# A GNN kernel's far tiles: one fused add and maximum per shared slot, and finer counts for GpSimd's lists

## The reference

```
h = relu(layernorm(x));  x = x + L0(h, adj)        # weighted mean of neighbours, times W
h = relu(layernorm(x));  x = x + L1(h, adj)        # hyperbolic mean
h = relu(layernorm(x));  x = x + L2(h, adj)        # maximum over 32 neighbours (below)
h = relu(layernorm(x));  x = x + L3(h, adj)        # hyperbolic mean with inverse roots of row sums

# L2
h = einsum('ni,oi->no', x, W) + b
_, topk_idx = top_k(adj, 32)          # the 32 largest entries of each row of adj
h_agg = max(h[topk_idx], axis=1)      # 8192 x 128
```

## Time and profile before

| | us |
|---|---|
| median of 3 runs | 3620.86 (3619.2 to 3623.95) |
| the profiled execution's own time | 3622.68 |
| its span, first to last instruction | 3620.9 |
| PE busy | 3338.5 (92%) |
| DVE busy | 2551.1 (70%) |
| POOL busy | 2505.2 (69%) |
| ACT busy | 1607.9 (44%) |
| gathers L508, own lists, whole program | 630.5, 624 instructions, 1010 ns each |
| rests L519 | 211.2, 485 instructions |

### The profile page before, as it was taken

How to read it: one execution, slowest core, us unless ns; L and a number is a source line. 1 busy time by engine, 2 the same in 40 slices (tenths; PEclk the granted TensorE clock), 3 DMA queues, 4 the chain that set the end, 5 groups by cost and what they waited for, 6 DMA issues and landing times.

```text
span 3620.9 us, 77053 instructions
## 1 busy us (share of the span) xinstructions
PE 3338.5 (92%) x29444; PEld 3316.9 (92%) x29444; DVE 2551.1 (70%) x5491; ACT 1607.9 (44%) x3554; POOL 2505.2 (69%) x2509
## 2 busy tenths in 40 slices
PE   6999999999999999999999999960899998999894
PEld 6999999999999999999999999960899998999894
DVE  6688888888888888530147656557787877878767
ACT  5777887887887887331222212222111111212124
POOL 3999998998998998200087666755787778778400
PEclk9999999999999999999999999985999999999997
DMA  6999999999999999888899999961788998889781
GB/s 211 393 397 389 387 379 367 385 382 361 390 382 367 388 386 365 312 292 293 289 342 331 327 329 333 329 233 39 268 306 303 321 323 305 296 310 337 269 291 57
DMA packets 401362, 1155.53 MB, mean 319 GB/s; under 512 B 36717, under 2 KB 56110, under 8 KB 401006
## 3 DMA queue, kind: packets, MB, share of 16 engines
q1 hardware_dynamic: 360096, 1082.21, 82.2%
q0 software_dynamic: 31360, 64.29, 5.8%
q10 hardware_dynamic: 9550, 4.69, 0.4%
HBM read 874.19 MB, written 276.86 MB: 318 GB/s over the span
## 4 chain that ended last, share of the span: by engine, by line
PE 65%; DVE 13%; POOL 12%; issue 5%; DMA 2%; ACT 2%; POOLq 0%; DVEq 0%; ACTq 0%; SPq 0%
PE psU L668 21%; PE psT L752 19%; PE psT L656 10%; POOL D L508 7%; PE psU L752 6%; PE psT L784 6%; POOL idle_end L519 2%; PE psU L784 2%; DVE agg L1695 2%; POOL ATS L508 2%; DMA adj_turned<-ATS 2%; DVE D L1482 1%; DVE HT L1691 1%; DVE W L1695 1%; DVE GR L1854 1%
## 5 line engine op out<-in xcount | busy, mean ns | idle before, releaser
L500 POOL TENSOR_TENSOR D<-D,iota 128x512 f32<-128x512 f32 x1024 | 1311.3, 1313 | 105.1 <-ACT D L911 83.9
L668 PE MATMUL psU<-HB,ATS 128*128 128x129 f32 x8192 | 1005.9, 276 | 18.7 <-ACT ATS L904 15.8
L668 PEld LDWEIGHTS psU<-HB,ATS 128*128 128x128 f32 x8192 | 957.0, 192 | 27.8 <-ACT ATS L904 19.9
L784 PE MATMUL psT<-ATS,PIECES 128*128 128x129 f32 x6144 | 787.3, 279 | 140.1 <-ACT ATS L1070 74.0
L784 PEld LDWEIGHTS psT<-ATS,PIECES 128*128 128x128 f32 x6144 | 741.4, 195 | 145.5 <-issue 113.4
L1482 DVE MAX8 D<-D 128x8 f32<-128x512 f32 x1024 | 643.0, 683 | 238.8 <-POOL D L500 231.0
L752 PE MATMUL psT<-GR,PIECES 128*128 128x129 f32 x6144 | 769.9, 275 | 1.1 <-issue 1.1
L508 POOL DMA_INDIRECT D<-h_table,idx_own x624 | 630.5, 1010 | 149.1 <-issue 101.4
L752 PEld LDWEIGHTS psT<-GR,PIECES 128*128 128x128 f32 x6144 | 727.2, 192 | 1.3 <-issue 1.3
L904 ACT ACTIVATE ATS<-psT 128x512 f32<-128x512 f32 x1024 | 555.7, 596 | 255.9 <-PE psT L656 208.5
L911 ACT ACTIVATE D<-PIECES 128x1024 f32<-128x1024 f32 x512 | 543.8, 1062 | 31.7 <-DVE D L1482 31.7
(11 more groups left out here) (411 smaller groups left out, 2739.1 us busy)
## 6 DMA issues: line engine op xcount, KB each, us to landing
PIECES<-adj_turned SPq DMA_DIRECT2D x512, 1024.0 KB
PIECES<-in_adj SPq DMA_DIRECT2D x256, 1024.0 KB
adj_turned<-ATS SPq DMA_DIRECT2D x512, 512.0 KB, 7.7
D<-h_table,idx_own POOLq DMA_INDIRECT x624
h_table<-HB ACTq DMA_DIRECT2D x8, 512.0 KB, 6.6
D<-h_table,idx_pool POOLq DMA_INDIRECT x215, 2.5
out_x<-X SPq DMA_DIRECT2D x3, 1024.0 KB, 5.1
ATS<-h_table,idx_pool POOLq DMA_INDIRECT x117
```

The costliest lines, as they stand in the source:

```text
L500: pool.tensor_tensor(key, key, iota[:, :], ALU.mult).then_inc(keyed, 1)
L668: last = nc.tensor.matmul(sum4(r), AT[K % NAT][:, b * GROUP + r * P:b * GROUP + (r + 1) * P], HB[:, j, :], start=(j == 0 and r % 2 == 0), ...
L784: last = nc.tensor.matmul(acc(h, r), block_of(slot, b, r), Hc[par][:, jj, :], start=(jj == 0 and opens(r)), stop=(jj == CT - 1 and closes(r)))
```

## The change

1. `far_tile` no longer reads n or branches. For each of the 22 slots, used or not, one SCALAR_TENSOR_TENSOR adds the mask's column to the slot and takes the maximum with an accumulator, alternately `gmax` and `pmax`; each waits for the one before last (`settle`). One maximum joins the two. Unused slots hold an earlier group's rows and are masked.
2. `pool_gathers` chooses its leaf by a binary tree of branches instead of a cascade; the far lists of groups 1 to 15 have twelve counts, `FAR_COUNTS`, instead of four. The near lists and the early group's keep their counts.

```
+FAR_COUNTS = [9, 10, 11, 12, 13, 14, 15, 16, 17, 18, 20, FAR_POOL]
...
-                if len(cuts) == 1:
-                    leaf(cuts[0])
-                    return
-                with pool.If(n < cuts[0] + 1):
-                    leaf(cuts[0])
-                with pool.Else():
-                    pool_gathers(ring, rows, index, n, cuts[1:], done, so_far, held)
+                def branch(counts):
+                    half = len(counts) // 2
+                    if not half:
+                        leaf(counts[0])
+                        return
+                    with pool.If(n < counts[half - 1] + 1):
+                        branch(counts[:half])
+                    with pool.Else():
+                        branch(counts[half:])
+
+                branch(cuts)
...
-                pool_gathers(far_pools[par], table, idx_pool[par], n, FAR_CUTS, far_pool_gathered[par],
+                pool_gathers(far_pools[par], table, idx_pool[par], n, FAR_COUNTS, far_pool_gathered[par],
...
-                n = dve.value_load(CTL[0:1, 1, g:g + 1], min_val=1, max_val=FAR_POOL)
+                ring, mask, best = far_pools[par], keep[par][:, r, :], (gmax, pmax)
                 dve.wait_ge(x_ready, t)
                 if r == 0:
                     dve.wait_ge(far_pool_gathered[par], 16 * FAR_POOL * ((g + 1) // 2))
                 dve.sem_inc(carrier["dve"], 1)
-                parts_max(t, n, FAR_CUTS, far_pools[par], far_kept, keep[par][:, r, :], gmax,
-                          NT + t * (TURNS // 2), NT + t * TURNS)
-                dve.wait_ge(pool_reduced, NT + (t + 1) * TURNS)
-                dve.sem_inc(carrier["dve"], 1)
+                for k in range(FAR_POOL):
+                    if k >= 2:
+                        settle(st.k - 1)
+                    mark(v.scalar_tensor_tensor(best[k % 2], ring[:, k, :], mask[:, k:k + 1],
+                                                best[k % 2] if k >= 2 else AGG[:, t, :], ALU.add, ALU.max))
+                settle()
+                link(v.tensor_tensor(gmax, gmax, pmax, ALU.max))
                 v.tensor_tensor(X[:, t, :], X[:, t, :], gmax, ALU.add).then_inc(x_ready, 1)
```

More of the change, by code:

```diff
@@ L225, in build @@
         KEPT = 2 * GROUP // P
-        far_kept = HT[:, :, :].rearrange("p b x -> p (b x)").rearrange("p (k f) -> p k f", f=P)
         gmax, pmax = agg4[:, 0, :], agg4[:, 1, :]
```

## The result

The changed kernel takes **3723.98 us** (median of 4 runs, 3718.65 to 3732.67) against 3620.43: ratio 1.0288, 95% interval 1.0269 to 1.0307. It is 103 us slower where 21 us faster were forecast. The profiled executions of the two kernels, from which their rows come, took 3719.05 and 3622.68, 96 us apart.

The account below looks back on a forecast made before the run. VectorE was taken to bind at long lists, with GpSimd a near second bound. GpSimd's last gather: 3402 - 16.8 - 20 + 48 = 3413, or 3409 chunk by chunk; so -21 us, 3600 us, range 3550 to 3642.

Parts of the forecast that it names:

- The bounds: Last stage: VectorE binds at long lists; GpSimd, 60.1 us a group against PE's 57.2, is only just ahead.
- the 79.2 us: Last stage: TensorE's time waiting, 32 times, for VectorE to free a PSUM buffer.
- Part 1, the merge: VectorE's far tiles: chain pitch 0.262 us, 7.8 us a tile for every list length, against 7.35 to 11.6.
- Rival C: VectorE's chain runs one after another, tile 10.5 us, VectorE binds in every chunk: +51, 3673 us; chance 0.05.
- Part 2, the lists: GpSimd's shared far lists: 218 gathers instead of 230, 1.40 us each, -16.8 us.
- Part 3, port contention: GpSimd's own gathers beside VectorE: fewer held as the long adds go, -20 us (between 0 and -33).
- Rival D: Port pair held through each VectorE chain: a gather waits some 4 us, 60 tiles, +240, about 3850 us; chance 0.02.
- Part 4, the jumps: GpSimd's list exits and entries: longer jumps over unused leaves miss instruction fetch, +48 us (bounds 0 and 103).
- The sum's method: Last stage: books of three engines kept chunk by chunk put GpSimd's last gather at 3409, the end at 3473 us.
- own gathers' mean under 1.0: Sign of being right: GpSimd's own gathers in the last stage average under 1.0 us, from 1.033.
- the wait on L784's buffers: Sign of being right: last-stage wait for PSUM buffers falls from 79 to under 20 us.
- gathers of 3 us or more (D): Sign of being wrong: GpSimd gathers taking 3 us or more, pointing to the port held through each chain.

Follow-up runs that it names:

- breaks6: Changed kernel with every sixth instruction of a tile's merge chain waiting for the one directly before it; 3612.87 us, ratio 0.9981.
- lists_only: Kernel before the change with only the finer list counts and the branch tree added, VectorE merging as before; 3640.23 us, ratio 1.0068.
- tails_psum: Changed kernel with merge accumulators in PSUM and the first 9 shared gathers placed ahead of the branch tree; 3541.82 us, ratio 0.9787.
- psum_acc: Changed kernel with the merge's two accumulators moved from SBUF to PSUM, tree and lists kept; 3602.87 us, ratio 0.9954.
- cuts_psum: Changed kernel with accumulators in PSUM and the old far lists (four counts, cascade of branches); 3564.88 us, ratio 0.9850.

## Why the prediction was wrong, point by point

- **The bounds** were read rightly, but for the 79.2 us, which count some waits twice: GpSimd just ahead of PE, VectorE binding at long lists. "The gain of a faster merge is soon capped by it" is what happened.
- **Part 1, the merge**: right. Pitch 0.262 forecast, 0.263 measured; tile 7.8 forecast, 7.71 measured, for every list. The 0.19 us an instruction estimated from the Trainium skill (page "VectorE: DVE Perf Modes", section on the TRN2 errata) is not what this chain shows. Rival C, a serial chain, is out. One reading was wrong without harm here: twelve instructions in 3.50 us are (3.50 - 0.345)/11 = 0.287 apart, not "the same" as 0.262. It does harm in part 3. (0.345 and 0.262 were each worked out from the other; the sixteen of the other chain last 0.346 us each and begin 0.262 apart.)
- **Part 2, the lists**: right. -16.8 us forecast; 218 shared gathers as counted from the inputs, and 15 us less of plain gather time.
- **Part 3, port contention: the step that failed.** Forecast -20 us, between 0 and -33; measured +94. GpSimd's last gather was put at 3413 and began at 3527, 114 us later, and this term alone was 114 us off. I rested it on one gather of 0.99 us beside a chain at 1950. That chain is not one row. The 0.287 above are pauses: the twelve stand in three rows of four, each 1.14 to 1.15 us long (two of them here), with a break before the next like those of breaks6.

```profile
1950.26 1.14 DVE L1647 SCALAR_TENSOR_TENSOR HB<-HB,OWNM,ATS 128x128 f32<-128x128 f32 x4 [0.16 <-DVE iota L1562]
...
1951.44 1.14 DVE L1647 SCALAR_TENSOR_TENSOR HB<-HB,OWNM,ATS 128x128 f32<-128x128 f32 x4
...
1952.92 0.95 POOL L508 DMA_INDIRECT D<-h_table,idx_own  x1 [0.31 <-issue]
```

The gather of 0.99 began 1.4 us into the chain but 0.2 us into a row of four, and even the next one, 2.7 us into the chain, took 0.95. All 15 chains at L1647 are broken in this way, so no row of the kernel before had a gather deep in an unbroken chain of this kind. The row could say nothing of 22 in a row, and the upper bound of the cost belonged at the chain's length, not at 0. Rival D named the mechanism and the place, but charged a wait of 4 us for each of 60 tiles, +240; 49 gathers took over 2 us, and +94 came of it. At 0.02 its chance was too low, and my range stopped at 3642.
- The Trainium skill's page "SBUF — State Buffer", section "Who interferes with whom", says that a VectorE instruction with two SBUF inputs contends with a GpSimd instruction that reads SBUF. The runs agree on the cause (140 us held with two SBUF inputs, 6.5 with one). They show an extent that was not in the forecast: of the gathers that come some 2 us or more into an unbroken row most are held, and then to the row's end.
- **Part 4, the jumps**: +48 forecast, +49 measured, also by place. Ahead of odd groups after an even exit +18 (21 forecast), behind odd groups' lists +9 (8.4), between own and shared lists +25 (18), and -2.5 at group 14, where GpSimd had waited for its index list before and, being later, no longer did; that was not foreseen. lists_only confirms it alone (+52), tails_psum that it goes with the length of the jumps (28 to 190 instructions out of a leaf instead of 158 to 428). By the Trainium skill (page "Runtime: NRT & Kernel Launch", section "Instruction fetch mechanics") a branch out of the fetched window stalls on a fetch. The counts agree: the new lists add 32 fetches of 8 KB, with the old merge (182 to 214) and with the new one (173 to 205).
- **The sum's method**: the books of the three engines hold when the terms do. psum_acc, which sets the failed term near its forecast, took 3603 against 3600, with the help of the two errors named there. cuts_psum was put at 3571 and took 3565.
- **Of the signs named**, "own gathers' mean under 1.0" failed at 1.31, the wait on L784's buffers rose to 172.9 us instead of falling from 79 to under 20, and "gathers of 3 us or more (D)" came true 46 times.

What is not settled: why gathers that begin in a chain's first 2 us get in. It depends on more than the time in the chain: of 24 that began at 2.02 or 2.03 us, 21 took 0.97 and 3 took 4.6.

## What to carry to other kernels

Before replacing a few long VectorE instructions with a long even chain, look at what GpSimd does beside it: keep all but one input of the chain out of SBUF (accumulators in PSUM cost nothing in pitch here and gave 121 us), or break it before it has run for 2 us (a break at every sixth instruction gave 111 us). Leaves of code that differ only in their count should share their common part ahead of the branch; a saving of 12 gathers was paid back threefold by the jumps over the unused leaves. And a row that shows an effect absent must be one where it would show: same length of unbroken chain, same place in it. Work out the pitch before calling two chains alike; here 0.287 against 0.262 gave the breaks away.

## What the runs showed of the hardware that was not expected

- A row of two-SBUF-input instructions 0.263 us apart can act as one for GpSimd's gathers, once it has run for some 2 us: a held gather ends 0.81 to 0.83 us behind the last of them, though each lasts 0.34 us. One break of 0.13 us in its middle took held time from 132 to 29 us, three took it to 18.
- What counts is the second input in SBUF. An output in SBUF with one SBUF input held nothing (6.5 us over 578 gathers).
- A SCALAR_TENSOR_TENSOR of 128x128 with its accumulator in PSUM runs at the same pitch (0.259) as in SBUF (0.263).
